# Wide cross attention: one key projection for two pairs of sequences, query and key projections in other places of the step, one split of the context per four sequences

## The reference, cut to what matters

```
q = layer_norm(x) @ wq2        # 128 tokens x 1280
k = context @ wk2              # 77 tokens x 1280
v = context @ wv2              # 77 tokens x 1280
attn = softmax(q k^T / 8) per head
x = concat(attn @ v) @ wo2 + bo2 + x
```

## Time and profile before

| What | us |
|---|---|
| median of three executions (lowest, highest) | 3690.57 (3687.29, 3707.21) |
| the profiled execution's own time | 3695.35 |
| its span in the trace | 3693.5 |
| stretch of the regular loop of the cross attention | 2405 to 3345 |
| one round of ten steps in it | 67.25 |

### The profile page before, as it was taken

The page is one execution under the profiler, slowest core; times in us unless marked ns, Lnnn a source line. Parts: engine busy times, 40 slices in busy tenths (PEclk is TensorE's granted clock), DMA queues, the critical chain, the costliest instruction groups (busy, mean ns, idle before and its releaser), DMA issues. The chain is left out here.

```text
span 3693.5 us, 98205 instructions
## 1 busy us (share of the span) xinstructions
PE 3606.9 (98%) x37983; PEld 3119.7 (84%) x37983; DVE 2315.9 (63%) x3922; ACT 2095.1 (57%) x5165; POOL 1252.6 (34%) x1273
## 2 busy tenths in 40 slices
PE   7999999999998999999999999899999999999999
PEld 5777778778887888898889888788888888888888
DVE  5788866664554666666666667555555555556554
ACT  3777777774445555555555555455555555555343
POOL 3333333332442333333333333333223222323342
PEclk7999999999999999999999999999999999999999
DMA  3444333232001000000000000000000000000000
GB/s 77 112 110 116 95 82 93 79 85 73 2 0 35 2 1 0 0 0 0 0 0 0 0 0 1 26 4 1 2 2 2 1 2 2 2 1 1 20 19 24
DMA packets 99546, 98.72 MB, mean 27 GB/s; under 512 B 31248, under 2 KB 74128, under 8 KB 99344
## 3 DMA queue, kind: packets, MB, share of 16 engines
q1 hardware_dynamic: 93408, 94.41, 9.9%
q0 software_dynamic: 5120, 1.35, 0.2%
q10 hardware_dynamic: 816, 0.08, 0.0%
HBM read 20.76 MB, written 5.24 MB: 7 GB/s over the span
## 5 line engine op out<-in xcount | busy, mean ns | idle before, releaser
L1213 POOL TENSOR_TENSOR a_probs<-a_probs,a_rsums 128x1024 f32<-128x1024 f32 x160 | 303.7, 1898 | 754.1 <-DVE a_rsums L1338 754.1
L1251 ACT ACTIVATE a_probs<-a_scores_banks,a_negmax 128x128 f32<-128x128 f32 x1280 | 367.4, 377 | 285.3 <-DVE a_negmax L1326 282.7
L1213 POOL TENSOR_TENSOR c_probs<-c_probs,c_rsums 128x616 f32<-128x616 f32 x160 | 204.6, 1279 | 757.4 <-DVE c_rsums L1338 757.3
L711 ACT ACTIVATE s_probs<-s_scoresT_banks 128x1024 f32<-128x1024 f32 (+1 forms) x320 | 327.4, 1023 | 193.1 <-PE s_scoresT_banks L895 190.8
L1251 ACT ACTIVATE c_probs<-c_scores_banks,c_negmax 128x77 f32<-128x77 f32 x1280 | 313.1, 335 | 197.4 <-DVE c_negmax L1326 197.2
L797 DVE TENSOR_REDUCE s_negmax<-s_scores_banks 128x8 f32<-128x1024 f32 (+1 forms) x320 | 322.3, 1007 | 147.7 <-PE s_scores_banks L877 143.3
L1319 DVE COPY c_outT<-c_out_bank 128x512 f32<-128x512 f32 x160 | 110.7, 692 | 367.6 <-PE c_out_bank L1498 307.2
L1319 DVE COPY a_outT<-a_out_bank 128x512 f32<-128x512 f32 x160 | 110.6, 692 | 293.9 <-PE a_out_bank L1498 240.7
L1667 DVE SCALAR_TENSOR_TENSOR f_hidden<-f_value_bank,bias,f_gate 128x512 f32<-128x512 f32 x160 | 120.1, 751 | 247.1 <-ACT f_gate L1642 245.2
L676 POOL DMA_DIRECT2D s_q_stack<-s_shift x160 | 93.6, 585 | 494.6 <-ACT s_shift L734 488.7
L1326 DVE TENSOR_REDUCE a_negmax<-a_scores_banks 128x4 f32<-128x512 f32 x320 | 206.1, 686 | 87.5 <-PE a_scores_banks L1397 87.5
(11 more groups left out here) (315 smaller groups left out, 10612.3 us busy)
## 6 DMA issues: line engine op xcount, KB each, us to landing
s_q_stack<-front SPq DMA_DIRECT2D x192, 160.0 KB, 3.3
s_k_stack<-front SPq DMA_DIRECT2D x96, 160.0 KB, 3.8
s_out<-s_heads SPq DMA_DIRECT2D x128, 80.0 KB, 2.4
s_k_stack<-front SPq DMA_DIRECT2D x96, 96.2 KB, 2.9
x_tokens<-in_x SPq DMA_DIRECT2D x16, 320.0 KB, 3.4
out_x<-x_tokens SPq DMA_DIRECT2D x16, 320.0 KB, 2.4
s_q_stack<-s_shift POOLq DMA_DIRECT2D x160, 8.0 KB, 2.6
s_ctx_in<-in_ctx SPq DMA_DIRECT2D x16, 115.5 KB
```

What stands on the lines that cost most here:

```text
L711: nc.scalar.activation(probs[i][0:NK, :, :], scoresT[0:NK, :, :], ACT.Exp).then_inc(s_exp, 1)
L1213: nc.gpsimd.tensor_tensor(probs[i][:], probs[i][:], rsums[(k - 1) % 2][:].unsqueeze(2).broadcast_to([P, UNIT, NK]), ALU.mult).then_inc(s_p ...
L1251: done = nc.scalar.activation(probs[i][:, h, :], scores[:, h // GROUP, h % GROUP * NK:(h % GROUP + 1) * NK], ACT.Exp, bias=negmax[k % 2][: ...
```

## The change

Only the cross attention is rewritten; self attention keeps its order (its context tiles are now halves of one wide tile). For the cross attention:

- Keys have a tile of their own, `keys`, of 4 contexts (308 columns) per 128 features. One key tile is projected for both pairs of a quad: 3 matmuls of 308 columns in the odd bank, 10 tiles per ten steps, at fixed places. `KEYS_EARLY` gives k and tile for those behind the queries, `KEYS_LATE` for those behind the output projection.
- Both query tiles of a unit go to the even bank (2 x 256 columns), right behind the scores, and ScalarE copies them as one of 512 columns, behind four exponentials.
- Values still go to the even bank, now behind output and late keys.
- The contexts of four sequences are loaded together at k = 0, transposed together at k = 5 behind the scores, cast and subtracted once as 308 columns. VectorE's subtraction is its first instruction in step k = 5.

```diff
+        KEYS_EARLY = {6: 1, 7: 2, 9: 4, 0: 5, 1: 6, 2: 7}
+        KEYS_LATE = {5: 0, 8: 3, 2: 8, 3: 9}
...
+        def keys_at(q, k, places):
+
+            t, double = places.get(k % BODY), q + (k + GROUPS) // BODY
+            return (t, double, double * TILES + t) if cross and t is not None and live(double, QUADS) else None
...
-                exponentials(q, k, 0, 6)
-                tile_out(q, k, 0)
-                exponentials(q, k, 6, 8)
-                tile_out(q, k, 1)
+                if cross:
+                    exponentials(q, k, 0, 4)
+                    query_out(q, k)
+                    keys_out(q, k, KEYS_EARLY)
+                    exponentials(q, k, 4, 8)
+                    keys_out(q, k, KEYS_LATE)
+                else:
+                    exponentials(q, k, 0, 6)
+                    tile_out(q, k, 0)
+                    exponentials(q, k, 6, 8)
+                    tile_out(q, k, 1)
                 values_out(q, k)
...
+                double = both_at(q, k)
+                if k == GROUPS and double is not None:
+                    dve.wait_ge(crossing.s_high, 2 * double + 2)
+                    nc.vector.tensor_tensor(ctx_low[0:CTX_D, :], odd_bank[0:CTX_D, 0:QUAD * NKC],
+                                            ctx_high[0:CTX_D, :].bitcast(F32), ALU.subtract).then_inc(s_ctx_split, 2)
...
+            def project_keys(q, k, places):
+
+                tile = keys_at(q, k, places)
+                if tile:
+                    t, double, order = tile
+                    if due(order):
+                        pe.wait_ge(s_k, order)
+                    if k % BODY in (3, 8):
+                        pe.wait_ge(done.s_y, 2 * (BASE + capped(pair_of(q, k) + 3, PAIRS)))
+                    if t == 0:
+                        pe.wait_ge(s_ctx_split, 2 * double + 2)
+                    kh, kl, ks = m.wparts[1]
+                    cols = slice(t * P, (t + 1) * P)
+                    ch, cl = ctx_high[0:CTX_D, :], ctx_low[0:CTX_D, :]
+                    products(nc, odd_bank[:, 0:QUAD * NK],
+                             [(kh[0:CTX_D, cols], ch), (kh[0:CTX_D, cols], cl), (kl[0:CTX_D, cols], ch)]).then_inc(s_kproj, 1)
...
+                if cross:
+                    project_queries(q, k)
+                    project_keys(q, k, KEYS_EARLY)
                 transpose_step(q, k - T_LAG)
                 output_step(q, k - Y_LAG)
-                project(q, k, 0)
-                project(q, k, 1)
+                if cross:
+                    project_keys(q, k, KEYS_LATE)
+                if not cross:
+                    project(q, k, 0)
+                    project(q, k, 1)
                 project_values(q, k)
                 values_step(q, k - T_LAG)
```

More of the change, by code:

```diff
@@ L462, in __init__ @@
         self.ctx_in = [sb(f"ctx_in{i}", [P, PAIR, CTX_D]) for i in range(2)]
-        self.high = [sb(f"ctx_high{i}", [P, PAIR * CTX_TOK], F32R) for i in range(2)]
-        self.low = [sb(f"ctx_low{i}", [P, PAIR * CTX_TOK], F32R) for i in range(2)]
+        self.high = sb("ctx_high", [P, QUAD * CTX_TOK], F32R)
+        self.low = sb("ctx_low", [P, QUAD * CTX_TOK], F32R)
         self.s_in = [m.semaphore(f"ctx_in{i}") for i in range(2)]
@@ L1109, in attention_wide @@
         done, BASE = norm.t, norm.offset
-        qk = sb("qk", [P, TILES, KCOL + PAIR * NK])
+        qk = sb("qk", [P, TILES, KCOL + (0 if cross else PAIR * NK)])
+        keys_two = sb("keys", [P, TILES, QUAD * NK]) if cross else None
         v = [sb(f"v{i}", [P, HEADS, dh]) for i in range(4)]
@@ L1188, in step @@
                     par = (k // GROUPS) % 2
-                    source = context(address(sp, seq_ahead(q, k) if cross else n * PAIR))
-                    if due(n - 1):
-                        sp.wait_ge(crossing.s_T, n - 1)
+                    source = context(n * PAIR)
                     sp.dma_start(crossing.ctx_in[par][0:NKC, :, :], source).then_inc(crossing.s_in[par], 16)
+                double = both_at(q, k)
+                if k == 0 and double is not None:
+                    sp.wait_ge(crossing.s_T, 2 * double)
+                    for par in range(2):
+                        sp.dma_start(crossing.ctx_in[par][0:NKC, :, :], context(address(sp, double * QUAD + par * PAIR)))\
+                            .then_inc(crossing.s_in[par], 16)
             sp.dma_start(m.wo[:, 0:TILES, :], wo.rearrange("(t p) n -> p t n", p=P)).then_inc(s_wo_in, 16)
@@ L1396, in scores_step @@
                             rows, t, col = slice(dh * j, dh * j + dh), 2 * g + c, (2 * c + a) * NK
-                            last = nc.tensor.matmul(scores[:, j, col:col + NK], qk[rows, t, a * P:(a + 1) * P],
-                                                    qk[rows, t, KCOL + a * NK:KCOL + (a + 1) * NK], start=True, stop=True)
+                            if cross:
+                                keys = keys_two[rows, t, (k // GROUPS * PAIR + a) * NK:(k // GROUPS * PAIR + a + 1) * NK]
+                            else:
+                                keys = qk[rows, t, KCOL + a * NK:KCOL + (a + 1) * NK]
+                            last = nc.tensor.matmul(scores[:, j, col:col + NK], qk[rows, t, a * P:(a + 1) * P], keys,
+                                                    start=True, stop=True)
                 last.then_inc(s_scores, 1)
@@ L1443, in project @@
                 elif g == 3:
[L1444 to L1446 removed]
+                    pe.wait_ge(done.s_y, 2 * (BASE + capped(n + 2, PAIRS + 2)))
                 elif g == 4 and isinstance(n, int) and n == PAIRS - 1:
@@ L1456, in project, with project_queries @@
                 keys = place[:, KCOL:KCOL + PAIR * NK]
-                if cross:
-                    ch, cl = ctx_high[par][0:CTX_D, :], ctx_low[par][0:CTX_D, :]
-                    last = products(nc, keys, [(kh[0:CTX_D, cols], ch), (kh[0:CTX_D, cols], cl), (kl[0:CTX_D, cols], ch)])
-                else:
-                    last = products(nc, keys, [(kh[:, cols], hh), (kh[:, cols], hl), (kl[:, cols], hh), (ks[0:STACK, cols], hs)])
-                last.then_inc(s_qkproj, 1)
+                last = products(nc, keys, [(kh[:, cols], hh), (kh[:, cols], hl), (kl[:, cols], hh), (ks[0:STACK, cols], hs)])
+                last.then_inc(s_qkproj, 1)
+            def project_queries(q, k):
+                tile = projection_at(q, k)
+                if not tile:
+                    return
+                g, n, par, r = tile
+                if g == 0:
+                    pe.wait_ge(done.s_split, BASE + n + 1)
+                if due(r):
+                    pe.wait_ge(s_v, r)
+                qh, ql, qs = m.wparts[0]
+                hh, hl, hs = norm.high[par][:], norm.low[par][:], norm.stack[par][0:STACK, :]
+                for i in range(2):
+                    cols = slice((2 * g + i) * P, (2 * g + i + 1) * P)
+                    last = products(nc, even_bank[:, i * KCOL:(i + 1) * KCOL],
+                                    [(qh[:, cols], hh), (qh[:, cols], hl), (ql[:, cols], hh), (qs[0:STACK, cols], hs)])
+                last.then_inc(s_qkproj, 1)
+            def project_keys(q, k, places):
+                tile = keys_at(q, k, places)
+                if tile:
+                    t, double, order = tile
+                    if due(order):
[9 more added lines that the diff above has]
+                             [(kh[0:CTX_D, cols], ch), (kh[0:CTX_D, cols], cl), (kl[0:CTX_D, cols], ch)]).then_inc(s_kproj, 1)
             def project_values(q, k):
@@ L1469, in project_values @@
                 g, n, par, r = tile
-                pe.wait_ge(s_qk, 2 * r + 1)
+                pe.wait_ge(s_qk, r + 1 if cross else 2 * r + 1)
+                if cross and k % BODY == GROUPS:
+                    pe.wait_ge(s_ctx_split, n + 2)
                 vh, vl, vs = m.wparts[2]
```

70 lines of the change are left out of this document (48 added, 22 removed).

## The result

| | before | after |
|---|---|---|
| median of 20 runs each, us | 3692.3 | 3657.45 |
| ratio to before, 95% interval | | 0.9916 [0.9897, 0.9935] |
| ten steps of the cross attention, us | 67.25 | 65.05 |

The changed kernel takes 0.84% less, 31 us by the ratio and 35 us by the two medians. I had put 3654 us and a range of 3636 to 3673.

The account below looks back on a forecast made before the run. TensorE's queue was taken to set the time. The terms -40.8 + 8 - 17.3 + 4.5 + 8.6 + 0.5 gave -36.5 us against the median 3690.57, so 3654 us, with a range of 3636 to 3673.

Parts of the forecast that it names:

- part 1: Key projection in the cross attention: 320 narrow tiles become 160 wide ones of 3 matmuls with 308 columns, -40.8 us.
- part 2: New neighbours of query and key blocks on TensorE start late, 0.05 us per step, +8 us.
- part 3: Old TensorE waits on the query copy (s = 3) and the context's low half (s = 4) go, -17.3 us.
- part 4a: At s = 3, values wait 0.15 us for the copy of both query tiles, 30 times, +4.5 us.
- part 4b: At k = 5, a serial VectorE and ScalarE chain holds values 0.47 and heads 0.10 us, +8.6 us.
- part 5: The rest: values wait 0.1 us in each of five steps ahead of the first scores, +0.5 us.
- part 4: The new waits that come in the cross attention: +4.5 us at s = 3 and +8.6 us at k = 5.
- R3: Rival: joins cost 0.15 us a step and the k = 5 wait is twice as long; 3679 us, chance 0.16.
- R1: Better rival: the new waits don't come and joins are free; -58 us, 3633 us, chance 0.14.
- R2: Rival: matmuls cost by their columns, so wide keys gain zero; 3695 us, chance 0.06.
- R4: Slower rival: queries wait each step for ScalarE's value copy, every step grows; 3709 us, chance 0.04.

Follow-up runs that it names:

- e1: Changed kernel with each key tile projected as two groups of 3 matmuls of 154 columns instead of one of 308: 3682.33 us, ratio 0.9970.
- b1: Kernel before with only its two waits removed (low-part subtraction behind the maxima, first query-tile copy behind four exponentials): 3678.13 us, ratio 0.9933.
- e4: Changed kernel with its two new waits removed (subtraction behind the maxima, query copy behind one exponential at s = 3): 3646.78 us, ratio 0.9877.
- e2: Changed kernel with queries and early keys moved behind the transposes of probabilities: 3658.09 us, ratio 0.9923.
- e6: Changed kernel with queries and early keys moved behind the output projection: 3739.57 us, ratio 1.0130.

## Why the prediction was right, point by point

The forecast held for its reasons in the main; some terms were mis-sized, and the errors were small against the sum and partly cancel.

| term | predicted | measured | from |
|---|---|---|---|
| part 1, wide keys | -40.8 | -34 | e1 |
| part 2, joins | +8 | +9 | e1 against before |
| part 3, waits that go | -17.3 | -21 | b1 |
| part 4a, s = 3 | +4.5 | +3.6 | e4 |
| part 4b, k = 5 | +8.6 | +8.7 | e4 |
| part 5, ahead of the loop | +0.5 | +1.4 | timeline |
| all | -36.5 | -33 | rounds, 15.5 x -2.20 = -34, and part 5 |

**Part 1** was right in kind and 7 us too large. The term that was mis-sized is the price of a narrow key matmul: I read 0.115 off the starts of the loads in the earlier trace rows, and by the difference of steps it is 0.107 (by the starts of the matmuls in e1, 0.105). The wide one was 0.143 where I had put 0.145. So 160 tiles at 0.21 make 34 us. In e1 only 26 of these show (1.65 us a round), since the waits at k = 3, 5 and 8 hide the rest; beside part 4, which was measured with wide tiles, the whole 34 belongs in the sum.

The terms can be set against each other in rounds. From b1 to e4, both free of such waits, ten wide tiles should bring -2.10 and ten joins +0.60, -1.50 together; measured is 64.23 - 65.84 = -1.61. The two new waits then bring 0.82, and -1.61 + 0.82 is the step from b1 to the changed kernel, -0.79. So the measured terms of the table, -32.3 in all, fall short of the rounds by 0.1 a round, some 1 to 2 us; where these lie stays open.

**Part 2** was right in size. I took 0.05 a step; the steps k = 0, 1, 6 and 7 of e1 are 0.05 to 0.06 longer than those of before with the same matmuls. I had the wrong join for the likely one, though: moving the queries away from the scores (e2) gave back 0.04 at most. R3, dear joins of 0.15, is out.

**Part 3** was too small by 4 us. In b1 both waits went, and the steps fell by 0.31 at k = 3, 0.23 at k = 8 and 0.44 at s = 4, more than the idle time in the profile (0.24 at k = 3, 0.37 at s = 4). The mis-sized term is the idle itself: a load of 128 lasts 0.19 us, but the next one starts 0.12 behind it when nothing holds it. The idle is counted from the load's end and so comes out 0.07 short of the delay: 0.24 + 0.07 and 0.37 + 0.07 are the 0.31 and 0.44.

**Part 4** is the part that I would point a learner to. The chain at k = 5 was worked out link by link from rows of a kernel that had no such step: values at 5.20 and heads at 6.14 behind the scores, so a step of 7.16. The profile after has 5.27, 6.14 and 7.16, and taking the subtraction out of the chain gives 0.58 back, where I had 0.57. At s = 3 the wait was 0.12 where I had 0.15.

That the figures meet so closely is in part luck. ScalarE's cast began at 1.70 where I had 1.62, and the subtraction at 2.21 in place of 2.03; but VectorE's next two instructions each began 0.07 to 0.09 before the one ahead had ended, which I had not counted, and the maxima began at 3.20 for my 3.19. On TensorE's side I put the four context transposes at 0.40, and they take 0.25. So TensorE would be at the output at 3.13, not 3.24 (e4 has it there), and it did wait for the copy of heads, a wait that I had put at nothing; it costs nothing in the sum, since the values are released later still. At the values TensorE would be at 4.61, not 4.73, so the wait there is 0.66 by starts, not 0.47, and the wait of 0.10 that I gave the heads hardly came (0.42 idle ahead of them, 0.40 in a step of before without any wait). The values take 0.87 behind their wait and 0.94 in e4. 0.47 + 0.10 and 0.66 - 0.07 happen to be nearly the same.

**Part 5** was 0.27 to 0.30 us in each of the five steps ahead of the loop (3.49 in place of 3.22), not 0.1.

**The rivals.** R1 (3633) failed on the wait at k = 5, which came. R2 fell with e1. The section Back-to-back issue gap of the Trainium skill's TensorE: Matmul & The Clock Gate gives 67 ns for a matmul of 154 columns and 131 for one of 308 as isolated gaps, and says itself that this gap counts no weight load and is too low for few columns. The runs agree with that warning: they show 107 and 143, with 128 weight columns loaded for every matmul. R4, the ring through ScalarE, did not come in the changed kernel: no idle ahead of the queries in any step. It did come, through the query copy in place of the value copy, once queries were put late (e6), at 0.43 us a step and with a total on the slow side.

Of what I said would show, a regular step with one key tile "near 6.2" is 6.32 and one without "near 5.8" is 5.89, both 0.1 too low. The round "near 64.8" is 65.05.

## What to carry to other kernels

Where TensorE's queue is full, read the starts of its weight loads block by block (and those of the matmuls where blocks of other widths meet); where the columns hardly move the price (0.107 us for 154 columns, 0.12 for 256), joining two matmuls into one of twice the width is worth it (six at 0.64 us became three at 0.43), but only in the steps where nothing else is late. Before widening, look for the one-line moves: work on a shared engine that stands ahead of something TensorE waits for, though nobody needs it yet. Such a chain can be added up link by link before it exists: here single links were off by up to 0.18 us and the instruction that the chain releases by 0.07.

## What the runs showed of the hardware

In one execution the granted clock went to 1.2 GHz for 102 us (459 to 562), in a stage where TensorE is busy nearly all the time: 102.45 of 103 us in the stretch itself, and 99.05 of the 101 us ahead of it (358 to 459) at the full clock. It cost about 37 us of that execution. The nine other profiles of this study show nothing of that length in that stage, and what brought it on is open. Whoever compares two kernels by their profiled spans alone would have called this change a loss of 4 us.
